# A four-model graph network on one core: in the attention scores, ScalarE waits for the store of gathered rows instead of VectorE

## The reference

```python
x_l = (x @ Wl + bl).reshape(n, H, C)
x_r = (x @ Wr + br).reshape(n, H, C)
e = (ea_f @ We).reshape(-1, H, C)
m = jax.nn.leaky_relu(x_l[src_f] + x_r[dst_f] + e, NEG_SLOPE)
alpha = jnp.einsum('ehc,hc->eh', m, att)
...
out = jax.ops.segment_sum(x_l[src_f] * alpha[..., None], dst_f, num_segments=n)
```

## Time and profile before

| | us |
|---|---|
| median of 3 runs | 5673.02 |
| lowest, highest run | 5667.77, 5698.64 |
| the profiled execution: its own time | 5635.86 |
| its span | 5634.0 |
| the scores, first one-hot to last score | about 2383 to 3572 |
| busy over the span: PE, DVE, POOL, ACT | 3155.7, 2758.5, 2030.6, 1580.4 |

### The profile page before, as it was taken

How to read it: one execution, slowest core, us unless ns; L and a number is a source line. 1 busy time by engine, 2 the same in 40 slices (tenths; PEclk the granted TensorE clock), 3 DMA queues, 4 the chain that set the end, 5 groups by cost and what they waited for, 6 DMA issues and landing times.

```text
span 5634.0 us, 59587 instructions
## 1 busy us (share of the span) xinstructions
PE 3155.7 (56%) x18327; PEld 2965.9 (53%) x18328; DVE 2758.5 (49%) x3804; ACT 1580.4 (28%) x2670; POOL 2030.6 (36%) x1982
## 2 busy tenths in 40 slices
PE   1300000009999999633333333167389999599697
PEld 0300000009989999632233223156289789589597
DVE  8300000024454444566667667888944244544345
ACT  0000000005645456200000000033266356356365
POOL 2777666750000000277777777256300000200300
PEclk9999999999999999855555555589799999799898
DMA  9700000008858588299999999257268178478685
GB/s 354 283 1 16 1 1 2 1 0 264 265 169 275 176 279 275 72 256 251 255 250 255 254 253 255 65 149 213 86 219 276 62 227 277 141 247 285 190 282 182
DMA packets 904091, 1037.25 MB, mean 184 GB/s; under 512 B 394307, under 2 KB 654361, under 8 KB 903878
## 3 DMA queue, kind: packets, MB, share of 16 engines
q1 hardware_dynamic: 811474, 890.08, 53.2%
q0 software_dynamic: 56208, 63.97, 4.8%
q10 hardware_dynamic: 36196, 80.53, 3.7%
HBM read 720.66 MB, written 233.37 MB: 169 GB/s over the span
## 4 chain that ended last, share of the span: by engine, by line
PE 43%; another core or an unknown queue 16%; DVE 12%; SPq 11%; issue 9%; DMA 6%; ACT 2%; DVEq 1%; POOL 0%; ACTq 0%; POOLq 0%
PE banks L939 35%; SPq L535 8%; DMA gathered<-work 5%; PE banks L862 4%; DVE work L1524 1%; DVE work L1401 1%; PE banks L1017 1%; SPq L514 1%; DVE Z L1323 1%; PE banks L884 1%; ACT X L689 1%; DVE big L1539 1%; DMA big<-cells 1%; DVE V L1132 1%
## 5 line engine op out<-in xcount | busy, mean ns | idle before, releaser
L939 PE MATMUL banks<-wides,rows 128*128 128x384 f32 (+2 forms) x11040 | 2028.6, 344 | 151.3 <-issue 65.9
L939 PEld LDWEIGHTS banks<-wides,rows 128*128 128x128 f32 x11040 | 1948.9, 189 | 225.3 <-issue 71.2
L645 POOL DMA_INDIRECT work<-tab,stage x832 | 882.7, 1061 | 1433.0 <-ACT stage L794 1141.8
L1284 DVE CAST wides<-big 128x768 fp32r<-128x768 f16 (+3 forms) x1429 | 811.3, 569 | 1176.0 <-PE banks L939 1067.9
L719 ACT CAST wides<-big 128x768 fp32r<-128x768 f16 (+2 forms) x1037 | 832.1, 804 | 674.2 <-PE banks L939 563.2
L619 POOL DMA_INDIRECT cells<-queue_i x784 | 786.2, 1003 | 309.1 <-issue 296.4
L989 PE MATMUL banks<-V,work 128*128 x1664 | 385.8, 424 | 802.1 <-issue 691.8
L989 PEld LDWEIGHTS banks<-V,work 128*128 128x128 f32 x1664 | 356.7, 325 | 831.1 <-issue 831.0
L671 POOL DMA_INDIRECT V<-tab,nodei x100 | 97.8, 978 | 1204.2 <-DMA tab<-X 879.7
L884 PE MATMUL banks<-work 128*128 128x50 f16 x784 | 92.7, 278 | 673.7 <-issue 609.9
L884 PEld LDWEIGHTS banks<-work 128*128 128x128 f16 x784 | 73.1, 149 | 693.2 <-issue 624.4
(11 more groups left out here) (298 smaller groups left out, 2933.1 us busy)
## 6 DMA issues: line engine op xcount, KB each, us to landing
big<-cells SPq DMA_DIRECT2D x490, 416.0 KB
big<-cells SPq DMA_DIRECT2D x441, 384.0 KB
big<-turned SPq DMA_DIRECT2D x300, 384.0 KB
gathered<-work SPq DMA_DIRECT2D x104, 512.0 KB
work<-gathered SPq DMA_DIRECT2D x104, 512.0 KB, 4.4
big<-turned SPq DMA_DIRECT2D x100, 416.0 KB
cells<-work ACTq DMA_DIRECT2D x98, 416.0 KB, 15.0
turned<-big SPq DMA_DIRECT2D x50, 800.0 KB
```

The source lines that it names most:

```text
L645: pool.indirect_dma_start(msg[:, j, u, :], None, tab[0][:, :], bass.IndirectOffsetOnAxis(ap=stage[:, j * U + u:j * U + u + 1].bitcast(U32) ...
L939: last = pe.matmul(banks[:, 4 * (w % 2) + j, 0:(z - a) * P], rows2[:, s, part * D:(part + 1) * D], wides[:, q % QUEUE, (a - start) * P:(z ...
L1284: dve.tensor_copy(wides[:, (2 * m + 1) % QUEUE, 0:(z - a) * P], halves[:, m % HALVES, a * P:z * P]).then_inc(s_wided, 1)
```

## The change

Three edits. SP adds 16 to each `s_store[j]` before its loop, so that the count is one store ahead. ACT, in front of its copy of the indices, waits for `s_store[j]` to reach i * 16 + 16, which by the new count is the store of group n-4, the last user of the slot. DVE no longer waits for the store in its loop; it waits for all four counts once after the loop.

```diff
@@ SP, before its loop over the groups
+            for j in range(RING):
+                sp.sem_inc(s_store[j], 16)
@@ ACT, in the scores
                     act.wait_ge(s_add, i * (RING * U) + (U * (j - RING + 1) + ADD0))
+                    act.wait_ge(s_store[j], i * 16 + 16)
                     act.copy(stage[:, j * U:(j + 1) * U], idxA[:, bass.ds(i * (RING * U) + j * U, U)]).then_inc(s_staged, 1)
@@ DVE, at the end of each group, and after the loop
                     dve.wait_ge(s_p1, at + 6)
-                    dve.wait_ge(s_store[j], i * 16 + 16)
                     dve.sem_inc(s_add, U)
             dve.wait_ge(s_add, U * GROUPS + ADD0)
+            for j in range(RING):
+                dve.wait_ge(s_store[j], ROUNDS * 16 + 16)
```

## The result

The changed kernel takes 5767.29 us (median of 4 runs, 5750.67 to 5785.33), against 5674.64 us before (4 runs): a ratio of 1.0156 with a 95% interval of 1.0113 to 1.0199. It is slower by some 93 us, where 35 us less was forecast.

What follows compares the result with a forecast made beforehand. The scores bound the kernel through a ring of SP's queue, DVE and the store, 11.51 us a group. 100 groups at 11.26 save 25 us, the end 10: 5673 - 35 = 5638 us, range 5595 to 5700.

Steps and rivals of the forecast that it cites:

- What is removed: DVE's stall for the store in front of the one-hot, 3.2 us a turn, goes, though not in full off the period.
- rival D: No change: DMA engines are full, period within 0.1 us of 11.51, time 5663 to 5675; chance 0.22.
- The turn of the freed queue: SP's time per group in the scores once DVE no longer holds it: 11.26 us against 11.51, range 9.8 to 12.34.
- gap and step: SP's time from save to transpose: 1.18 us from save to row load, then 0.49 for load and step.
- landing: Time from the end of the transpose's issue to SP's next save: 3.46 us, upper end 3.82.
- The 15 early turns: Groups before the change with save-to-load gaps under 2.25 us; their averages gave issue 6.13 us and landing 3.46.
- C: Slower: transposes crowded by moving save and row load, 12.34 us a group, 73 us more, 5746; chance 0.14.
- Group 41: The single earlier group with the freed queue's short gap: transpose issue 6.16 us, save to save 11.45, cited against slowing.
- The deciding sign: The transposes' median issue on SP after the change: 5.0 us says Rival B, 6.1 A, 6.8 and more C.
- A: The prediction's own sum: 11.26 us a group in the scores, 35 us less, 5638 us; chance 0.42.
- Rival B: POOL's gathers become the bound in the scores: floor 10.97 us a group, 64 us less, 5609; chance 0.22.
- The end: Last score some 11 us behind POOL's last gather instead of 21.2: 10 us less, or 0 if DVE stays behind.

Runs made afterwards that it cites:

- e5: The changed kernel again, unaltered, on the experiments' chip, against the kernel before: ratio 1.0178, 5307.74 us.
- e8: The changed kernel with SP's row load issued behind the transpose instead of in front of it, against the kernel before: ratio 0.9898.
- e9: The kernel before, DVE still waiting for the store, with the row load issued behind the transpose: ratio 0.9871 against the kernel before.
- e16: The changed kernel with the row load behind the transpose and the four increments in front of SP's first strips: ratio 0.9843 against the kernel before, 5136.91 us.
- e1: The changed kernel with DVE's wait for the store put back beside ACT's new one: ratio 1.0024 against the kernel before.
- e12: The changed kernel without transposes and saves in the scores, semaphore increments in their place: ratio 0.9906 against the kernel before.
- e11: The kernel before without transposes and saves in the scores, semaphore increments in their place: ratio 0.9873 against the kernel before.
- e15: The changed kernel with the four increments moved in front of SP's first strips: ratio 1.017 against the kernel before.
- e10: The changed kernel without the row loads inside the loop: ratio 0.988 against the kernel before.
- e2: The changed kernel, with SP also waiting before each transpose until the previous group's save has landed: ratio 1.0043 against the kernel before.
- e4: The changed kernel with the saves of groups j = 0, 1, 2 of each turn issued one group later: ratio 0.9929 against the kernel before.

## Why the prediction was wrong

- **What is removed.** Right: the stall for the store went (308.6 us), and the freed load follows the save at once, 0.90 us at the median where I took 1.18. That DVE's idle time would move to the next row was named in rival D, and it did: 384.1 us.
- **The turn of the freed queue, 11.26 us.** This is the step that failed. Of its terms, gap and step were 1.67 and measured 1.76; the issue was 6.13 and measured 6.22; the **landing was 3.46 and measured 4.41**, above even the 3.82 that I had set as its upper end. On the chip of the experiments (e5) the gap was shorter, 1.22, and issue (6.78) and landing (4.48) both outran their terms. So the mechanism stood in the text and its size was wrong.
- **The 15 early turns behind these terms** (group 41, set apart there, is a sixteenth) were of two kinds, and their average hid it. Ten followed an ordinary turn (issue 4.8 to 5.0 us): they took 6.6 us to issue and 3.7 to land, as means. The other five (groups 6, 15, 23, 31, 67) followed a turn whose own issue had been 6.1 us or more, and were ordinary again: 5.1 and 3.0. Groups 66 and 67 are one of each:

```profile
3148.95 0.34 SPq L514 DMA_DIRECT2D big<-rel_rows  x1
3149.45 7.43 SPq L535 DMA_TRANSPOSE big<-cells  x1
...
3160.66 0.36 SPq L528 DMA_DIRECT2D turned<-big  x1
3162.81 0.34 SPq L514 DMA_DIRECT2D big<-rel_rows  x1
3163.30 5.02 SPq L535 DMA_TRANSPOSE big<-cells  x1
```

With the ten alone the sum is 1.67 + 6.6 + 3.7 = 12.0 us, past the 11.89 from which C decides. That an early turn could be ordinary again behind a crowded one did not carry over to the free queue: in e5 none of the 95 transposes issues in under 5.6 us. All 15 had the load at least 2.15 us behind the save, where e5 has 0.64 at the median. Whether that is the difference, no run shows; nor can the turn before be told from the slot, since all ten were in slot 2 and four of the five in slot 3 (in e5 slot 2 issues in 7.03 us and slot 3 in 6.46).
- **Group 41 as the witness against C.** It had 3.62 us of landing and followed a disturbed turn, as the text warned. It was the wrong sample to bound with.
- **The deciding sign** was the median issue: 6.1 us for A, 6.8 and more for C. The first profile has 6.32, which reads as nearer to A. The sign left out the landing, where most of the miss was.
- **Rival C** was right in place and near in price: 12.34 us a group against 12.39 measured, 73 us against 93. It had 0.14. That its sum for a group came so near is in part luck: it took 6.85 for the issue and 3.82 for the landing, and they were 6.22 and 4.41. The rule that I set beside it, that the descriptors of POOL and those of SP feed different queues in the same engines, which take turns (the Trainium skill, "DMA: Bandwidth & Descriptors", "SWDGE vs HWDGE vs iDMA"), was not what cost: in e8 POOL gathers without a pause and the turn is short.
- **Rival D** falls: e8 moves 269 GB/s. The DMA share of 1.01 was no ceiling; it reaches 1.13.
- **Rival B's floor**, 10.97 us, was near: the gathers of groups 5 to 99 run at 10.7 to 10.9 us a group in e8, e9 and e16. But the change alone doesn't lead there; it takes SP's order as well.
- **The edits costed at 0.** ACT's wait in the loop costs nothing (e1). The four increments on SP don't: I looked at what they are and not at what they stand behind. They cost 17 us in e12 against e11 and 22 or more in e8 against e16. In the changed kernel itself the crowded queue hides them: e15 is level with e5 within the noise. e1's 13 us fit them, but no run settles that.
- **The end.** Right: the last score is 10.9 us behind POOL's last gather (3686.17 to 3697.11), where it was 21.2.

## What to carry to other kernels

A stall that also paces a shared DMA queue is not free time: before you remove it, ask what the queue will issue sooner, and into which transfers. Where a small load sits in front of a long transfer and waits for a compute engine, move it behind: here that order alone gave 1.2 to 1.3%, the wait's new place alone lost 1.6%, and both together, with the increments early, gave 1.6% (0.4% more than the order alone beside it). An increment that gives a semaphore a head start belongs where nothing stands in front of it.

## What the runs showed of the hardware that was not expected

- The issue time of the same DMA transpose on SP, 24 or 25 blocks of 128 x 128, goes from 3.5 us (e10) and 3.7 us (e2), where it starts 4.1 to 4.2 us behind the save, to 5.0 before, 6.3 to 6.7 in the changed kernel and 7.4 in e4 (medians). It is no fixed cost of the instruction.
- A transfer of half the bytes in front of the transpose costs nearly as much as the whole (12.16 against 12.49 us a turn), and the transpose's issue is as long with either (6.81 and 6.78). Why one more transfer in that place weighs so much stays open; no run here looks inside the queue.
- The DMA share is 1.01 at 253 GB/s before, 1.08 at 234 GB/s in e5 and 1.13 at 269 GB/s in e8. So a share of 1.0 doesn't mean full, and a higher share doesn't mean that more is moved.
